# Attention with linear features and a routed expert layer: the increment of the state goes second and the scores last in a step's first run of 64-row matmuls, the rank behind both last projections

## The reference

```python
h = layernorm(x) * (1 + ca) + sa
q, k, v = heads(h @ wq.T), heads(h @ wk.T), heads(h @ wv.T)     # 16 heads of 64
phi = lambda t: exp(t @ omega.T - 0.5 * sum(t * t)) / 8          # 64 features
out = phi(q) . cumsum(phi(k) v) / (phi(q) . cumsum(phi(k)) + 1e-6)
x = x + ga * (out @ wo.T + bo)
h = layernorm(x) * (1 + cb) + sb
scores = softmax(h @ wg); the best 2 of 8 experts, at most 1024 rows each, in order of row
x = x + gb * sum of the two experts' gelu(row @ w1 + b1) @ w2 + b2, weighted
```

## Time and profile before

| | |
|---|---|
| median of 3 runs | 747.66 us (746.46 to 751.94) |
| the profiled execution | 750.19 us, span of its records 748.4 us |
| TensorE busy | 712.3 us (95%) |
| VectorE, ScalarE, GpSimd busy | 547.2, 384.3, 337.6 us |
| a step of the first stage | 16.96 us |

### The profile page before, as it was taken

The page is one execution under the profiler, slowest core; times in us unless marked ns, Lnnn a source line. Parts: engine busy times, 40 slices in busy tenths (PEclk is TensorE's granted clock), DMA queues, the critical chain, the costliest instruction groups (busy, mean ns, idle before and its releaser), DMA issues. The chain is left out here.

```text
span 748.4 us, 27606 instructions
## 1 busy us (share of the span) xinstructions
PE 712.3 (95%) x11581; PEld 613.6 (82%) x11581; DVE 547.2 (73%) x1684; ACT 384.3 (51%) x740; POOL 337.6 (45%) x630
## 2 busy tenths in 40 slices
PE   7989999999999999999999999999998679999996
PEld 6878888888888888888888888888887669999994
DVE  6477888888888888788888788878775445655427
ACT  4555566556665556655566555655552134445310
POOL 3002444545555544444555554444446504565550
PEclk9799999999999999999999999999999999999999
DMA  9982000000000000000000000000000054454128
GB/s 259 363 314 90 9 10 11 10 10 11 9 11 13 14 10 10 11 9 10 10 11 10 10 17 9 11 10 10 10 10 10 25 169 144 135 175 137 50 83 296
DMA packets 32707, 47.27 MB, mean 63 GB/s; under 512 B 4132, under 2 KB 20168, under 8 KB 32584
## 3 DMA queue, kind: packets, MB, share of 16 engines
q1 hardware_dynamic: 23296, 32.62, 13.0%
q0 software_dynamic: 4096, 8.42, 3.5%
q10 hardware_dynamic: 5192, 4.47, 1.8%
HBM read 22.21 MB, written 23.36 MB: 61 GB/s over the span
## 5 line engine op out<-in xcount | busy, mean ns | idle before, releaser
L1265 POOL DMA_INDIRECT y_rows<-y_sb,row_id x64 | 62.8, 982 | 66.6 <-DVE y_sb L1409 50.6
L639 ACT COPY v_sb<-bank 128x512 f32<-128x512 f32 x64 | 37.6, 588 | 106.9 <-PE bank L279 103.5
L1009 POOL TENSOR_TENSOR h_lo<-h_full,h_hi 128x192 fp32r<-128x192 f32 x32 | 19.1, 597 | 141.2 <-ACT h_hi L632 141.2
L1079 POOL DMA_INDIRECT dispatched<-h_cur,slot x64 | 67.2, 1050 | 17.9 <-issue 16.1
L1343 ACT ACTIVATE hidden<-bank,b_col 128x512 f32<-128x512 f32 x64 | 43.3, 689 | 58.2 <-PE bank L1316 57.8
L623 ACT ACTIVATE phi_k<-expo_k 128x1024 f32<-128x1024 f32 x32 | 33.9, 1058 | 62.8 <-DVE expo_k L754 62.8
L515 PEld LDWEIGHTS bank<-woT,attT 128*128 128x128 f32 x512 | 61.9, 191 | 3.1 <-ACT attT L725 0.6
L515 PE MATMUL bank<-woT,attT 128*128 128x128 f32 x512 | 62.4, 275 | 0.4 <-ACT attT L725 0.4
L1285 PE MATMUL bank<-w_sb,hidden 128*128 128x128 f32 x512 | 59.7, 275 | 0.8 <-issue 0.8
L1285 PEld LDWEIGHTS bank<-w_sb,hidden 128*128 128x128 f32 x512 | 58.4, 192 | 1.2 <-issue 1.2
L754 DVE SCALAR_TENSOR_TENSOR expo_k<-norm_k,bank 128x512 f32<-128x512 f32 x64 | 44.0, 687 | 19.3 <-PE bank L279 19.2
(11 more groups left out here) (236 smaller groups left out, 2084.7 us busy)
## 6 DMA issues: line engine op xcount, KB each, us to landing
dispatched<-blank SPq DMA_DIRECT2D x16, 524.0 KB, 3.0
region<-dispatched SPq DMA_DIRECT2D x30, 262.0 KB, 2.9
y_rows<-blank SPq DMA_DIRECT2D x8, 512.0 KB, 3.5
w_nat<-in_L_ffn_w_dram SPq DMA_DIRECT2D x8, 256.0 KB, 3.5
y_got<-y_rows SPq DMA_DIRECT2D x8, 256.0 KB, 6.8
y_got<-y_rows ACTq DMA_DIRECT2D x8, 256.0 KB, 7.7
out_dram<-x_sb SPq DMA_DIRECT2D x8, 256.0 KB, 3.5
w_sb<-in_L_ffn_w_dram ACTq DMA_DIRECT2D x6, 256.0 KB, 3.2
```

Source lines behind the costliest of these rows:

```text
L1079: pool.indirect_dma_start(out=dispatched[:, :], in_=h2_cur[par][:], in_offset=None, out_offset=bass.IndirectOffsetOnAxis(ap=slot[par][:, k ...
L1265: pool.indirect_dma_start(out=y_rows[:, :], out_offset=bass.IndirectOffsetOnAxis(ap=row_id[par][:, t:t + 1].bitcast(U32), axis=0), in_=y_s ...
```

## The change

In TensorE's step the increment moves from the end of the first run to its second place and the score 0 moves behind attend, so that both scores stand last. VectorE's state_add 0 goes ahead of normalise 1. The rank goes behind pk1, and VectorE's find_places behind the second expo_k.

```diff
 if tail:
     attend_state(1, c - 1, nxt, (j - 1) % CPB)
-score(0, c, par)
+state_gain(0, c, par, j)
 if tail:
     attend(1, c - 1, nxt, (j - 1) % CPB)
+score(0, c, par)
 score(1, c, par)
-state_gain(0, c, par, j)
...
 if front:
     project("pk0", c, nxt)
+    project("pk1", c, nxt)
 if last:
     routing_rank(c)
-if front:
-    project("pk1", c, nxt)
...
 if front:
     sum_squares("k", c)
+if back:
+    state_add(0)
 if tail:
     normalise(1, c - 1)
 if back:
-    state_add(0)
     mask(0)
     mask(1)
...
 if front:
     exponent("k", 0, c)
+    exponent("k", 1, c)
 if last and c != NCH:
     find_places()
-if front:
-    exponent("k", 1, c)
```

## The result

The changed kernel takes 738.92 us, the median of four runs (737.82 to 739.69); the kernel before took 747.56 beside them. By the medians that is 8.6 us or 1.2% faster; the ratio of the runs is 0.9866 with a 95% interval of 0.9833 to 0.9899. The forecast was 736.6, with 729.5 to 743.5 as its range.

What follows compares the result with a forecast made beforehand. TensorE was taken to bound the steps, with only its order's waste to gain: 11.4 + 1.2 - 1.5 = 11.1 us off, 750.19 to 739.1 profiled, 736.6 on the median; range 729.5 to 743.5.

Steps and rivals of the forecast that it cites:

- TensorE bounds the steps, by starts and not by busy time: Attention-stage steps of 16.96 us: TensorE, busy 16.80, is the limit; busy time hides waste, so block starts are read.
- The order of the first run: TensorE's first run of 64-row matmuls: increment and attend cover the phiT_k wait; 0.38 us a step (0.22 to 0.46), 11.4 us.
- The slow fifth block belongs to the place: First run's fifth block, the increment, takes 0.08 us more from its place in a long run; the score inherits it.
- The rank: Rank matmuls moved behind pk1 on TensorE: 0.04 us a step (bounds 0 and 0.09), x29 steps = 1.2 us.
- 1.5 us given back for instruction packets: In 4 first runs the phiT_k wait may have hidden an instruction wait: 4 x 0.38 = 1.5 us taken back.
- the slower rival: Instruction supply gives out: each packet in a first run costs a 0.9 us wait; at worst 760 us; chance 0.05.
- the paced run: Instructions pace the first run: 0.22 us in 30 steps, no rank gain, 5.1 us off, 742.6 us; chance 0.20.
- Its own signs: Right: L308's wait gone, first run 2.5 to 2.6 us, steps about 16.55, pk matmuls 1.49; wrong: first run above 2.75.
- full cover: The fifth block's slowness is the increment's own and no packet shows: 16.4 us off, 731.3 us; chance 0.17.

## Why the prediction was right, and which term was off

- *TensorE bounds the steps, by starts and not by busy time*: right. VectorE and ScalarE never came into it, and undoing VectorE's part changed nothing. What came into it unforeseen were GpSimd's issues of indirect DMAs.
- *The order of the first run*: the mechanism was right, the wait for phiT_k is gone with 0.6 us of margin. The size was off: 0.38 a step was taken, and 0.23 measured in most steps, near the lower bound of 0.22. The 30 runs gave 7.8 us instead of 11.4. With the indirect DMAs out of the way the order is worth 0.40 (2.89 to 2.49); order and DMAs together are worth 0.47 (2.965 to 2.49), the upper bound.
- *The slow fifth block belongs to the place*: this step failed in its reason. The prediction put it down to a supply of instructions that a long run uses up, and carried 0.08 over to the score. What the runs showed: it goes with GpSimd's issues of indirect DMAs, and is gone when they are moved. In the kernel before the first issue came right behind the pause and left no gap. Without the pause it costs 0.19 in the attend block and the run 0.25 in all. Whether the second issue adds to these 0.25 isn't shown: with the rank last there is a step (from 220.20 on) in which the second comes behind the run, and the run took 2.75 all the same. The row that would have told it, GpSimd at 207.19 and 208.62, was in the trace and wasn't read, since GpSimd "waits for none of the moved rows".
- *The rank*: 1.2 us taken, nothing seen (3.34 and 3.35 us in the traces; the ratio of 0.9994 alone couldn't tell). The prediction's own doubt was right: pk1 gets its 0.08 back and the heads' projection takes 0.09 more, and the lower bound of 0 was the value.
- *1.5 us given back for instruction packets*: not seen apart from the rest. The "issue" waits on TensorE in the first stage were 3.7 us before (1.5, 1.5, 0.7) and 3.4 after (1.9, 1.3, 0.2): no more, so the slower rival (each packet in a run costs a wait) didn't come.
- *The sum*: 11.1 us were forecast and 8.6 measured. Of the 10.4 between the two profiled executions 7.8 came from where they were said to; 1.3 lie ahead of the steps, and nothing in the change accounts for them. So that the time lies well inside the range is in part luck: the largest term came out a third smaller than forecast, and the lower bound that most steps kept to came from a reason that failed. Of the rivals the paced run (742.6) had the size of the first term right for most steps and, like the forecast, gave a reason that the runs didn't bear out.
- *Its own signs*: the wait of L308 is gone and the six pk matmuls take 1.50. But the first run of 2.74 is above the 2.5 to 2.6 of "right" and just under the 2.75 of "wrong", the steps are 16.75 and not 16.55, and the slow block was the third and not the fifth, which neither reading of the fifth block foresaw.
- *A reading of the clock line*: not the first but the second 40th of the span has the lower clock (9, then 7). It lies ahead of the steps and changes nothing in the sum.

The Trainium skill's rule, that crossing an instruction block is mostly hidden (Runtime: NRT & Kernel Launch, section Instruction fetch mechanics), stood in the prediction beside full cover. The slow blocks don't speak against it: they went with the indirect DMAs, though no run tells whether those act through the fetch. Of the 78 instruction packets most pass without a long wait, in agreement with the rule. Four don't: the four gaps of 0.86 to 1.06 us in the starts of TensorE's matmuls between 60 and 560 us each end 1.2 to 1.5 us behind the landing of a 16 KB packet (for one, 328.57 and 327.24). These four aren't hidden.

## What to carry to other kernels

Read a run of short matmuls by the starts of its blocks, and compare a block with the same code at another place: two runs of one shape with different times mean that something beside them differs. Where several variants keep a delay at different blocks but the same total, list its moment against every instruction of the other engines, those that nobody waits for too. A constant distance names a suspect; moving the suspect is the test. Then look for steps with the suspect and without the delay. And put GpSimd's indirect DMAs beside wide matmuls, not beside runs of short ones: here that was worth 0.25 us in most steps of the changed kernel, as much as the change itself, and 0.08 in the kernel before.

## What the hardware showed that wasn't expected

While GpSimd issued an indirect DMA, TensorE's short matmuls paused for 0.09 to 0.17 us; the pause mostly ended 0.62 to 0.64 us behind the start of the issue, though the two share no tile, no bank and no semaphore at that point. Moved to 204.45, beside projections of 512 columns, the issue shows nothing there: they keep starting 0.23 us apart. It showed nothing, either, shortly behind a pause of TensorE or a block with half the matmuls. By what way it acts (the memory, the queue, the sequencer, the supply of instructions) no run here tells. One wait instruction more on TensorE inside such a run cost 0.1 us, yet one less gave nothing while the DMA's gap was there; without the gap it wasn't tried. A pair of 16-column bf16 matmuls between others costs 0.06 us itself and some 0.09 beside it: in what follows at the first two places, in the heads' projection ahead of it at the third.
